# A mixture-of-experts kernel: token pairs fetched one product group earlier, sums of y reordered, constant matmuls in the head

## The chip, the cores and the metric

The kernel runs on one core of a Trainium2 chip. The metric is the device time of one execution in microseconds (us); lower is better. The engines are TensorE (PE), VectorE (DVE), ScalarE (ACT) and GpSimd (POOL); SyncE (SP) only issues DMA transfers.

## The reference

`x` has 4 x 1024 tokens of width 512. A rotation of four 128-wide parts (quaternions, with a gate per channel) is applied to each token, then a mixture of experts: 8 experts, each token goes to its best 2, each expert takes at most 1024 tokens, and its two layers are 512 x 2048 and 2048 x 512.

```python
x_rotated = hamilton(q_left_n, hamilton(x_filtered, q_right_conj))
scores = softmax(xf @ gate_w.T); topv, topi = top_k(scores, 2)
loc = place of the token in its expert; valid = loc < cap
h = relu(einsum('ecd,ehd->ech', de, fc1_w) + fc1_b)
eo = einsum('ech,ehd->ecd', h, fc2_w) + fc2_b
out = x + sum(gathered * gates * w)
```

## The kernel before

Everything is float32, and each product is made of three float32r matmuls: each operand is split in a high part (ACT copies it to float32r) and a low part (DVE subtracts), and high x high, high x low and low x high are added up (L1002 to L1004, L1025 to L1030). The first layer is done by a Strassen-Winograd scheme with seven products instead of eight on 2 x 2 blocks.

**Head** (up to about 118 us): logits, top 2, the slot of each token, and tables of rows (`gather_row`). The tokens of expert 0 are gathered, turned on TensorE, rotated from PSUM (`rotate_ps`, L792) and combined to the sums of y (`y_sum`, L751), of which `y_high` (ACT, L454) and `y_low` (DVE, L767) make the two parts.

**Each expert e** then has 32 steps of the second layer, and 8 groups of the first. A *group* g makes two tiles of the hidden layer: seven `product` calls (six matmuls each), and two calls of `fc2` (twelve each) for tiles of the group before. After the groups come 16 *tiles*, in which TensorE only does `fc2`. In these tiles DVE and ACT also make the sums of y of the next expert. The order of each engine's work is written out by hand in its block; semaphores tie them together.

**Tokens of the next expert** come in four *pairs* of blocks V = 4e .. 4e+3, each two blocks of 128 tokens, through one buffer `x_blk`:

1. POOL gathers the two blocks from `in_x` (`gather_x`, L345), after DVE has turned the pair before (`cut_T`), and writes them to a scratch `slots_dram` in HBM;
2. SP reads them back in another cut, by eight DMAs (`cut_x`, L265, through `load_cut`), once the write has landed (`cut_out`);
3. DVE waits for them (`cut_in`) and transposes them (`turn_x`, L772); ACT makes the first term of the rotation (`first_of_slab`, L469) and DVE adds the three others (`rotate`, L783).

Before the change DVE turns pair 0 in group 0, pair 1 in group 1, pair 2 late in group 4 and pair 3 in group 5. In a group, `turn_x` stands before the sum that releases TensorE's last product (L877, `c22_done`, waited for at L1095):

```python
if g < 2: turn_x(4 * e + g)
...
dve.wait_ge(s3_ready, G + 1)
dve.scalar_tensor_tensor(h1[:, 2 * g + 1, :], ps[:, BANK_P5, :], bias[1], s3[:, :], ...).then_inc(c22_done, 1)
```

SP also loads the weights in one queue: `load_w2` (one DMA each, three buffers; step N+3 is loaded when `w2_ready` shows step N used) and `load_w1` (eight DMAs for a group). The w2 steps 0, 1 and 2 of the next expert are asked for in tiles 13, 14 and 15. POOL's queue also holds `gather_rows` and `scatter_rows` of the output (L365, L372), which add a slab's result to `out`, and the gates.

In the first group of an expert ACT copies the first w2 step to its high part (`w2_high`, L448) before it copies `s3` (L535), for which TensorE's product A22 waits.

## Time and profile before

| | us |
|---|---|
| median of 3 runs (lowest, highest) | 1586.12 (1583.0, 1586.63) |
| the profiled execution's own time | 1586.64 |
| its span in the trace | 1584.9 |

The profile is of one execution. Its first part gives the busy time of each engine, its second the span in 40 slices (busy share in tenths, granted TensorE clock, DMA). TensorE is busy for 1416.6 us (89%), DVE for 1074.1 us (68%), ACT for 709.3 us (45%), POOL for 383.0 us (24%). Matmul records overlap, so that a matmul's 0.39 us is its length and not its distance to the next; distances are read from starts.

### The profile page before, as it was taken

The numbers are of one execution on the slowest core, as the hardware profiler recorded it, in microseconds if no ns is written. First come the engines' busy times: TensorE is split into PE (matmuls) and PEld (weight loads), VectorE is DVE, ScalarE is ACT, GpSimd is POOL, SyncE is SP. The second block draws the span as 40 slices with busy tenths as digits, with TensorE's granted clock in tenths as the row PEclk, the third lists the DMA queues.
The fourth block names the chain that finished last, engine by engine and source line by source line (L and its number), as shares of the span: only waits on it lengthen the run. The fifth ranks groups of instructions, "written<-read, shape, count | busy, mean of one in ns | idle before, by whom it ended". The sixth has DMA issues, their size and how long they took to land.

```text
span 1584.9 us, 17933 instructions
## 1 busy us (share of the span) xinstructions
PE 1416.6 (89%) x6095; PEld 1148.1 (72%) x6095; DVE 1074.1 (68%) x1632; ACT 709.3 (45%) x1072; POOL 383.0 (24%) x322
## 2 busy tenths in 40 slices
PE   8548989979898899979899798989899798999997
PEld 5326867868776778758778587767788587788885
DVE  6786758656685768747686567847587476866543
ACT  5234445434463435444454344634454444544442
POOL 1061112520052210531025200522105310240011
PEclk9667999989999899989999899999999899999999
DMA  8465464564555554564635645555545635354232
GB/s 314 155 146 120 81 137 98 168 141 93 115 135 159 118 125 90 153 162 85 141 106 168 132 94 116 142 151 117 125 93 153 156 81 103 103 167 81 52 94 92
DMA packets 452141, 200.45 MB, mean 126 GB/s; under 512 B 398816, under 2 KB 401001, under 8 KB 450130
## 3 DMA queue, kind: packets, MB, share of 16 engines
q1 hardware_dynamic: 429922, 132.27, 37.4%
q0 software_dynamic: 22128, 67.03, 13.6%
q8 instruction: 49, 0.80, 0.2%
q14 instruction: 42, 0.34, 0.1%
HBM read 159.50 MB, written 39.98 MB: 126 GB/s over the span
## 4 chain that ended last, share of the span: by engine, by line
PE 62%; DVE 14%; DMA 11%; SPq 4%; issue 4%; POOL 3%; ACT 1%; DVEq 0%; POOLq 0%; ACTq 0%
PE ps L1025 11%; PE ps L1026 11%; PE ps L1030 11%; PE ps L1002 9%; PE ps L1004 8%; PE ps L1003 8%; DMA x_blk<-in_x,gather_row 4%; SPq L228 4%; DMA slots_dram<-x_blk 3%; DMA x_blk<-slots_dram 2%; DVE w_lo L745 2%; POOL rows L368 1%; DVE yfull L801 1%; DVE yfull L789 1%; DVE h L816 1%
## 5 line engine op out<-in xcount | busy, mean ns | idle before, releaser
L1002 PE MATMUL ps<-yc_hi,w1c_hi 128*128 128x512 f32 x896 | 360.9, 403 | 103.1 <-DVE h L877 100.7
L1025 PE MATMUL ps<-w_hi,h_hi 128*128 128x512 f32 x960 | 383.3, 399 | 4.1 <-issue 2.4
L1026 PE MATMUL ps<-w_lo,h_hi 128*128 128x512 f32 x960 | 380.2, 396 | 0.0
L1003 PE MATMUL ps<-yc_lo,w1c_hi 128*128 128x512 f32 x896 | 357.7, 399 | 0.0
L1004 PE MATMUL ps<-yc_hi,w1c_lo 128*128 128x512 f32 x896 | 357.7, 399 | 0.0
L1002 PEld LDWEIGHTS ps<-yc_hi,w1c_hi 128*128 128x128 f32 x896 | 173.2, 193 | 147.7 <-DVE h L877 106.6
L1030 PE MATMUL ps<-w_hi,h_lo 128*128 128x512 f32 x960 | 256.8, 389 | 0.0
L1025 PEld LDWEIGHTS ps<-w_hi,h_hi 128*128 128x128 f32 x960 | 186.1, 194 | 49.6 <-issue 5.3
L1026 PEld LDWEIGHTS ps<-w_lo,h_hi 128*128 128x128 f32 x960 | 185.2, 193 | 39.2
L1030 PEld LDWEIGHTS ps<-w_hi,h_lo 128*128 128x128 f32 x960 | 180.5, 188 | 37.9
L1004 PEld LDWEIGHTS ps<-yc_hi,w1c_lo 128*128 128x128 f32 x896 | 173.6, 194 | 37.2
L1003 PEld LDWEIGHTS ps<-yc_lo,w1c_hi 128*128 128x128 f32 x896 | 173.9, 194 | 35.6
L745 DVE TENSOR_TENSOR w_lo<-w_raw,w_hi 128x512 fp32r<-128x512 f32 x256 | 175.4, 685 | 19.2 <-ACT w_hi L452 19.1
L376 POOL DMA_INDIRECT out<-rows,scatter_row x32 | 83.3, 2602 | 416.1 <-DVE rows L816 408.8
L452 ACT ACTIVATE w_hi<-w_raw 128x512 fp32r<-128x512 f32 x256 | 159.7, 624 | 46.4 <-PE ps L1030 41.2
L740 DVE TENSOR_TENSOR w1c_lo<-w1t,w1c_hi 128x1792 fp32r<-128x1792 f32 x64 | 129.6, 2026 | 35.1 <-ACT w1c_hi L446 33.1
L446 ACT ACTIVATE w1c_hi<-w1t 128x1792 fp32r<-128x1792 f32 x64 | 109.2, 1706 | 91.4 <-DVE w1t L736 79.8
L350 POOL DMA_INDIRECT x_blk<-in_x,gather_row x56 | 54.5, 972 | 385.2 <-DVE x_turned L780 361.9
L806 DVE SCALAR_TENSOR_TENSOR h_lo<-ps,h_hi 128x512 fp32r<-128x512 f32 x64 | 44.2, 690 | 138.2 <-ACT h_hi L530 131.3
L780 DVE STREAM_TRANSPOSE x_turned<-x_blk 128x512 f32<-128x512 f32 x56 | 36.5, 690 | 145.7 <-DMA x_blk<-slots_dram 145.7
L789 DVE SCALAR_TENSOR_TENSOR yfull<-x_turned,rot,yfull 128x512 f32<-128x512 f32 x168 | 114.8, 747 | 0.0
L489 ACT ACTIVATE ps<-ps,b1T 128x512 f32<-128x512 f32 x64 | 42.3, 662 | 152.9 <-PE ps L1004 128.5
(160 smaller groups left out, 1578.2 us busy)
## 6 DMA issues: line engine op xcount, KB each, us to landing
w_raw<-in_L_ffn_fc_w SPq DMA_DIRECT2D x256, 256.0 KB
w_raw<-in_L_ffn_fc_w SPq DMA_DIRECT2D x512, 64.0 KB
slots_dram<-x_blk POOLq DMA_DIRECT2D x28, 512.0 KB
x_blk<-slots_dram SPq DMA_DIRECT2D x224, 64.0 KB
out<-x_all SPq DMA_DIRECT2D x8, 1024.0 KB, 12.6
x_all<-in_x SPq DMA_DIRECT2D x7, 1024.0 KB, 13.3
b_bc<-in_L_ffn_fc_b POOLq DMA_DIRECT2D x8, 256.0 KB
x_all<-in_x SPq DMA_DIRECT2D x4, 256.0 KB, 3.9
```

The lines of the kernel that those rows point to most:

```text
L376: pool.indirect_dma_start(out_rows, bass.IndirectOffsetOnAxis(ap=scatter_row[:, at:at + 1], axis=0), slab_rows[s % 2][:, b, :], None, boun ...
L446: act.activation(w1c_hi[:, G % 2, :, :], w1t[:, 1:8, :], ACT.Copy).then_inc(w1_hi_ready, 1)
L452: act.activation(w2_hi[:, N % 3, :], w2_raw[:, N % 3, :], ACT.Copy).then_inc(w2_hi_ready, 1)
L740: dve.tensor_tensor(w1c_lo[:, G % 2, :, :], w1t[:, 1:8, :], w1c_hi[:, G % 2, :, :].bitcast(F32), ALU.subtract).then_inc(w1_ready, 1)
L745: dve.tensor_tensor(w2_lo[:, N % 3, :], w2_raw[:, N % 3, :], w2_hi[:, N % 3, :].bitcast(F32), ALU.subtract).then_inc(w2_ready, 1)
L789: ins = dve.scalar_tensor_tensor(y, x_turned[:, :, j, :], rot[:, i, j:j + 1], y, ALU.mult, ALU.add)
L1002: pe.matmul(bank, hi, yc_hi[:, y, q, :], start=first and q == 0, stop=False, skip_group_check=True)
L1003: pe.matmul(bank, hi, yc_lo[:, y, q, :], start=False, stop=False, skip_group_check=True)
L1004: ins = pe.matmul(bank, lo, yc_hi[:, y, q, :], start=False, stop=last and q == 1, skip_group_check=True)
L1025: pe.matmul(eo_s[:, b, :], h_hi[:, c, blk], w2_hi[:, w, :], start=False, stop=False, skip_group_check=True)
L1026: pe.matmul(eo_s[:, b, :], h_hi[:, c, blk], w2_lo[:, w, :], start=False, stop=False, skip_group_check=True)
L1030: ins = pe.matmul(eo_s[:, b, :], h_lo[:, c, blk], w2_hi[:, w, :], start=False, stop=False, skip_group_check=True)
```

## The change

Parts of it, by place:

- **SP.** From expert 1 on, the reload of pair 1 stands in tile 12 of the expert before, not at the end of group 0. In expert 0 the reloads of pairs 2, 3 and 4 move to group 3, the end of group 5 and tile 1.
- **POOL.** `gather_x(4e+5)` (pair 1 of the next expert) moves in front of `scatter_rows(2e+1)`.
- **DVE.** Pair 0 is turned in tile 10 of the expert before (in the head for expert 0), pair 1 in group 0, pair 2 late in group 3, pair 3 in group 5 as before. In expert 0 these stand one group later (`lag`). The sums of y have another order and other buffers: T3's sum goes to y12, T1's to the turned blocks, T4's to y21; the low parts of B11 and B21 come ahead of sums 1 and 2.
- **ACT.** The first terms of the rotation are made in groups 0 and 5 (1 and 6 in expert 0). In the head the copies for T4 and B22 and the biases of the output banks are made inside group 0.
- **PE.** In the head 28 matmuls whose result nobody reads (`keep_warm`) stand after product p2, and the four that prepare the output banks wait for the rotation only.

```diff
@@ sync
-                    if not last and g == 2:
+                    if not last and g == (2 if e else 3):
                         cut_x(4 * e + 2)
-                    if e < E - 2 and g == 6:
+                    if 0 < e < E - 2 and g == 6:
                         cut_x(4 * e + 4)
...
-                    if not last and g == 0:
-                        cut_x(4 * e + 1)
-                    if not last and g == 4:
+                    if e == 0 and g == 0:
+                        cut_x(1)
+                    if not last and g == (4 if e else 5):
                         cut_x(4 * e + 3)
...
+                    if e == 0 and tile == 1:
+                        cut_x(4)
+                    if e < E - 2 and tile == 12:
+                        cut_x(4 * e + 5)
@@ gpsimd
+                if e == 0:
+                    gather_x(1)
                 if not last:
-                    gather_x(4 * e + 1)
                     gather_x(4 * e + 2)
...
                 gather_rows(2 * e + 1)
+                if e < E - 2:
+                    gather_x(4 * e + 5)
                 scatter_rows(2 * e + 1)
@@ scalar
+                    if G == 0:
+                        y_high(0, T4, 4, y21)
+                        y_high(0, B22, 0, y22)
                     w2_high(N)
...
-                    if not last and g == 1:
+                    if not last and g == (0 if e else 1):
                         first_of_slab(e + 1, 0)
...
                         if tile == 6:
-                            y_high(e + 1, T2, 3, y11)
+                            y_high(e + 1, T2, 2, y11)
                         if tile == 7:
-                            y_high(e + 1, T3, 1, t3)
+                            y_high(e + 1, T3, 3, y12)
@@ vector
             rotate_ps(1)
+            rotate_ps(2)
             y_low(0, B11, y11)
             y_low(0, B21, y21)
-            rotate_ps(2)
             rotate_ps(3)
...
+            turn_x(0)
...
+                    lag = 0 if e else 1
                     if not last:
-                        if g < 2:
-                            turn_x(4 * e + g)
-                        elif g < 5:
-                            rotate(e + 1, 0, g - 1)
-                        elif g == 5:
+                        if g == lag:
+                            turn_x(4 * e + 1)
+                        if lag < g < 4 + lag:
+                            rotate(e + 1, 0, g - lag)
+                        if g == 5 + lag:
                             turn_x(4 * e + 3)
...
-                    if not last and g == 4:
+                    if not last and g == 3 + lag:
                         turn_x(4 * e + 2)
...
                         if tile == 1:
+                            if lag:
+                                rotate(e + 1, 1, 3)
                             y_sum(e + 1, 0)
...
-                        if tile == 3:
+                        if tile == 5:
                             y_sum(e + 1, 1)
...
-                        if tile == 5:
+                        if tile == 6:
                             y_sum(e + 1, 2)
...
+                        if tile == 10 and e < E - 2:
+                            turn_x(4 * e + 4)
@@ tensor
                     if G == 0:
                         p2(G)
+                        keep_warm(28)
+                        pe.wait_ge(rotated, rotated_by(0, 1, 6))
+                        set_bits(range(EO[0], EO[0] + SB))
```

POOL's queue around the end of expert 1, before. The first row is the scatter of the first slab, then come the bias row, the gather and scatter of the second slab's rows, the gather for the next expert's first slab, and a pair of token blocks with its write.

```order
L376 DMA out<-rows,scatter_row 4096x512 x4
L384 DMA b_bc<-in_L_ffn_fc_b 128x512
L368 DMA h<-out,gather_row 128x512 x4
L376 DMA out<-h,scatter_row 4096x512 x4
L368 DMA rows<-out,gather_row 128x512 x4
L350 DMA x_blk<-in_x,gather_row 128x512 x2
L355 DMA slots_dram<-x_blk 128x2x512
```

The same place with the change:

```order
L380 DMA out<-rows,scatter_row 4096x512 x4
L388 DMA b_bc<-in_L_ffn_fc_b 128x512
L372 DMA h<-out,gather_row 128x512 x4
L354 DMA x_blk<-in_x,gather_row 128x512 x2
L359 DMA slots_dram<-x_blk 128x2x512
L380 DMA out<-h,scatter_row 4096x512 x4
L372 DMA rows<-out,gather_row 128x512 x4
```

The pair's two gathers and its write have moved ahead of the second slab's scatter, behind the four gathers of `h`.

SP's queue at the turn from expert 1 to expert 2, before: 18 w2 loads (16 in the tiles, of which the last three are the next expert's steps 0, 1 and 2, and 2 in its group 0), then group 0's w1, the reload of pair 1, and group 1's loads.

```order
L263 DMA w_raw<-in_L_ffn_fc_w 128x512 x18
L228 DMA w_raw<-in_L_ffn_fc_w 32x16x32 x8
L228 DMA x_blk<-slots_dram 32x16x32 x8
L263 DMA w_raw<-in_L_ffn_fc_w 128x512 x2
L228 DMA w_raw<-in_L_ffn_fc_w 32x16x32 x8
```

With the change:

```order
L263 DMA w_raw<-in_L_ffn_fc_w 128x512 x13
L228 DMA x_blk<-slots_dram 32x16x32 x8
L263 DMA w_raw<-in_L_ffn_fc_w 128x512 x5
L228 DMA w_raw<-in_L_ffn_fc_w 32x16x32 x8
L263 DMA w_raw<-in_L_ffn_fc_w 128x512 x2
```

The reload of pair 1 now stands in front of the last five w2 loads, three of which are the next expert's steps 0, 1 and 2.

DVE in tiles 5, 6 and 7 of expert 1, before (L806 and L745 are the low parts of h and w2 that each tile needs; L761 is `y_sum` 2, L769 a `y_low`):

```order
L806 SCALAR_TENSOR_TENSOR h_lo<-h,h_hi 128x512
L745 TENSOR_TENSOR w_lo<-w_raw,w_hi 128x512
L761 TENSOR_TENSOR yfull<-yfull 128x2x512
L806 SCALAR_TENSOR_TENSOR h_lo<-h,h_hi 128x512
L745 TENSOR_TENSOR w_lo<-w_raw,w_hi 128x512
L769 TENSOR_TENSOR yc_lo<-yfull,yc_hi 128x1024
```

With the change (L816 and L754 are these low parts, L768 is `y_sum` 1, L771 `y_sum` 2):

```order
L816 SCALAR_TENSOR_TENSOR h_lo<-h,h_hi 128x512
L754 TENSOR_TENSOR w_lo<-w_raw,w_hi 128x512
L768 TENSOR_TENSOR yfull<-yfull,x_turned 128x2x512
L816 SCALAR_TENSOR_TENSOR h_lo<-h,h_hi 128x512
L754 TENSOR_TENSOR w_lo<-w_raw,w_hi 128x512
L771 TENSOR_TENSOR yfull<-yfull 128x2x512
```

A sum stands in tile 6 as well, where a low part stood; ACT's copy of its result stands in tile 7.

## Rows read from the trace of the kernel before

**Rows 1.** The page, part 2: the span in 40 slices.

```profile
PEclk9667999989999899989999899999999899999999
...
GB/s 314 155 146 120 81 137 98 168 141 93 115 135 159 118 125 90 153 162 85 141 106 168 132 94 116 142 151 117 125 93 153 156 81 103 103 167 81 52 94 92
```

**Rows 2.** Waits of PE over the span: us in total, times, longest us.

```profile
PE ps L1002 <- DVE h L877: 100.7, 14, 11.4
```

**Rows 3.** Busy times by stretch: expert 1, and expert 7 (clock is next to last).

```profile
303.00:487.00 184.00, 168.44 (x720) 137.50 (x719) 127.11 (x187) 84.54 (x127) 48.18 (x37) 0.95 0.55 128
...
1408.00:1571.50 163.50, 163.50 (x723) 135.40 (x723) 85.97 (x130) 68.70 (x106) 18.50 (x16) 1.00 0.35 89
```

**Rows 4.** Timeline of PE, expert 1: start, us, what [idle before <- releaser].

```profile
335.58 0.79 PE L1002 MATMUL ps<-yc_hi,w1c_hi 128*128 128x512 f32 x1 [10.24 <-DVE h L877]
...
339.10 0.39 PE L1025 MATMUL ps<-w_hi,h_hi 128*128 128x512 f32 x1
...
402.08 0.79 PE L1002 MATMUL ps<-yc_hi,w1c_hi 128*128 128x512 f32 x1 [4.75 <-DVE h L877]
...
407.34 0.39 PE L1025 MATMUL ps<-w_hi,h_hi 128*128 128x512 f32 x1
```

**Rows 5.** Timeline of DVE, expert 1, the turns of pairs 1 and 3.

```profile
333.59 1.30 DVE L780 STREAM_TRANSPOSE x_turned<-x_blk 128x512 f32<-128x512 f32 x2 [12.53 <-DMA x_blk<-slots_dram]
...
400.09 1.30 DVE L780 STREAM_TRANSPOSE x_turned<-x_blk 128x512 f32<-128x512 f32 x2 [8.88 <-DMA x_blk<-slots_dram]
```

**Rows 6.** Timelines of POOL and SP, expert 1: gather, write, reload.

```profile
322.94 0.76 POOL L355 DMA_DIRECT2D slots_dram<-x_blk  x1 [5.60 <-DMA x_blk<-in_x,gather_row]
...
382.52 0.95 POOL L350 DMA_INDIRECT x_blk<-in_x,gather_row  x1 [29.28 <-DVE x_turned L780]
...
389.46 0.75 POOL L355 DMA_DIRECT2D slots_dram<-x_blk  x1 [4.74 <-DMA x_blk<-in_x,gather_row]
...
326.15 5.55 SPq L228 DMA_DIRECT2D x_blk<-slots_dram  x8
```

**Rows 7.** Timelines of PE and SP, head and expert 0.

```profile
118.44 2.08 PE L1036 MATMUL ps<-yc_hi,w1c_hi 128*128 128x512 f32 x4 [9.97 <-DVE yc_lo L769]
...
148.88 0.80 PE L1002 MATMUL ps<-yc_hi,w1c_hi 128*128 128x512 f32 x1 [4.44 <-DVE h L877]
...
217.84 0.80 PE L1002 MATMUL ps<-yc_hi,w1c_hi 128*128 128x512 f32 x1 [6.11 <-DVE h L877]
...
138.64 5.72 SPq L228 DMA_DIRECT2D x_blk<-slots_dram  x8
```

**Rows 8.** Timelines of DVE, ACT and PE, expert 1: rotation, tiles 6 and 7.

```profile
441.14 2.73 DVE L789 SCALAR_TENSOR_TENSOR yfull<-x_turned,rot,yfull 128x512 f32<-128x512 f32 x4
...
458.77 0.69 DVE L806 SCALAR_TENSOR_TENSOR h_lo<-h,h_hi 128x512 fp32r<-128x512 f32 x1 [1.70 <-ACT h_hi L583]
...
457.16 1.06 ACT L460 ACTIVATE yc_hi<-yfull 128x1024 fp32r<-128x1024 f32 x1 [5.36 <-DVE yfull L761]
...
462.98 0.39 PE L1025 MATMUL ps<-w_hi,h_hi 128*128 128x512 f32 x1
```

**Rows 9.** Timelines of POOL and DVE, expert 1, tiles 8 to 12.

```profile
464.91 6.54 POOL L368 DMA_INDIRECT h<-out,gather_row  x1 [0.30 <-issue]
...
473.01 1.36 POOL L368 DMA_INDIRECT h<-out,gather_row  x1 [0.30 <-issue]
...
472.26 0.69 DVE L806 SCALAR_TENSOR_TENSOR h_lo<-h,h_hi 128x512 fp32r<-128x512 f32 x1 [1.70 <-ACT h_hi L583]
...
474.77 0.69 DVE L806 SCALAR_TENSOR_TENSOR h_lo<-h,h_hi 128x512 fp32r<-128x512 f32 x1 [1.22 <-ACT h_hi L583]
```

**Rows 10.** Timelines of PE and ACT, expert 1, group 0.

```profile
303.17 0.39 PE L1002 MATMUL ps<-yc_hi,w1c_hi 128*128 128x512 f32 x1
...
312.81 0.47 PE L1002 MATMUL ps<-yc_hi,w1c_hi 128*128 128x512 f32 x1
...
309.31 0.62 ACT L452 ACTIVATE w_hi<-w_raw 128x512 fp32r<-128x512 f32 x1
```

More of the change, by code:

```diff
@@ L167, in program @@
         x0_rows = h1[:, 0:2 * SB, :]
-        t3 = x_turned[:, 0:2, :, :].rearrange("p b q n -> p (b q n)").rearrange("p (k n) -> p k n", k=2)
+        t1 = x_turned[:, 0:2, :, :].rearrange("p b q n -> p (b q n)").rearrange("p (k n) -> p k n", k=2)
         slab_rows = (rows[:, :, :], h1[:, ROWS1:ROWS1 + SB, :])
@@ L506, in _ @@
             seed_c11(0)
-            y_high(0, T2, 3, y11)
-            y_high(0, T3, 1, t3)
-            y_high(0, T1, 2, y12)
-            act.wait_ge(bits_set, 2)
-            for b in range(SB):
-                seed_eo(0, b)
-            y_high(0, T4, 4, y12)
-            y_high(0, B22, 0, y22)
+            y_high(0, T2, 2, y11)
+            y_high(0, T3, 3, y12)
+            y_high(0, T1, 1, t1)
             for e in range(E):
@@ L536, in _ @@
                     w2_high(N + 1)
+                    if G == 0:
+                        act.wait_ge(bits_set, 2)
+                        for b in range(SB):
+                            seed_eo(0, b)
                     if g < GROUPS - 1:
@@ L551, in _ @@
                         w1_high(G + 2)
-                    if not last and g == 1:
+                    if not last and g == (0 if e else 1):
                         first_of_slab(e + 1, 0)
-                    if not last and g == 5:
+                    if not last and g == (5 if e else 6):
                         first_of_slab(e + 1, 1)
@@ L774, in turn_x @@
                 if u == 0:
-                    dve.wait_ge(yc_ready, 7 * e)
+                    dve.wait_ge(yc_ready, 7 * (e - 1) + T1 + 1)
                 if u == 2:
@@ L1037, in set_bits, with keep_warm @@
                 ins.then_inc(bits_set, 1)
+            def keep_warm(count):
+                for n in range(count):
+                    pe.matmul(ps[:, BANK_P5, :], w1c_hi[:, 0, A11, 0:P], yc_hi[:, B11, 0, :], start=True, stop=True)
             def p1(G):
@@ L1065, in _ @@
                         p2(G)
+                        keep_warm(28)
+                        pe.wait_ge(rotated, rotated_by(0, 1, 6))
+                        set_bits(range(EO[0], EO[0] + SB))
                     if g == 0:
                         pe.wait_ge(yc_ready, 7 * e + T2 + 1)
-                    if G == 0:
-                        set_bits(range(EO[0], EO[0] + SB))
                     pe.wait_ge(c11_seeded, G + 1)
```

45 lines of the change are left out of this document (22 added, 23 removed).

## The prediction, made before the change was run

> **What bounds the kernel now.** I read the clock and rate by slice first, then PE's waits, then the stretches of single experts, then the timelines around the longest waits. The granted clock [rows 1] is at 0.9 or more nearly everywhere, with dips of 0.8 that come twice per expert. PE's waits [rows 2] have one large entry: 14 waits, 100.7 us in all, for DVE's sum at L877. Fourteen is two for each of the seven experts that fetch tokens for a next one. The stretches [rows 3] (behind each total come PE, PEld, DVE, ACT and POOL busy, then clock, DMA share and GB/s) show the price: expert 1 does its 720 matmuls in 184 us at a clock of 0.95, expert 7, which fetches nothing, does 723 in 163.5 at 1.00. That is 0.2267 us from start to start, so 163.2 us is the floor of an expert and some 21 us of each are lost. PE bounds the kernel, and what it waits for decides.
>
> In expert 1 PE stops for 10.24 us in group 1 and 4.75 us in group 5 [rows 4]. DVE at these places waits 12.53 and 8.88 us at the head of a turn, for the reload from the scratch [rows 5]; the sum at L877 stands behind it in DVE's queue. So DVE has 2.3 us of slack in group 1 and 4.1 us in group 5. The fetch itself is a chain [rows 6]: from the first gather (382.52) to the write (389.46) 6.9 us, longer when other gathers are in the queue; 3.2 us from the write (322.94) to the reload's start (326.15); 5.55 us to issue its eight DMAs, and the data are there at 333.59 [rows 5], 7.4 us after that start. About 18 us in all, against a group of 15 us (66 matmuls). After each stop the clock is low: the eight matmuls from 335.58 to 339.10 take 3.5 us instead of 1.8, and the twelve from 402.08 to 407.34 take 5.3 instead of 2.7 [rows 4]. That adds 1.7 and 2.5 us.
>
> **What the change removes.** In experts 1 to 6 pair 1 is asked for in group 0, but its buffer is free since tile 10 of the expert before; that stop goes from group 1. Pair 2 is turned late in group 3, pair 3 in group 5, so pair 3 has nearly two groups. Its reload now comes out behind group 4's w1 in SP's queue. By my chain w1 is issued from 381.7 to 387.4 in the old trace's time, the reload starts there, lands at 394.9, and DVE asks at 391.2: a wait of 3.7 us against the slack of 4.1 us [rows 4, 5]. I take 0.3 us for PE, between 0 and 1.
> Stops removed: 100.7 minus the 4.44 of expert 0's group 1 [rows 7], which stays: **96.3**. Low clock behind them: 6 x (1.7 + 2.5) + 2.5 for expert 0's group 6: **27.7**.
>
> **The head and expert 0.** Pair 1 of expert 0 is still asked for in group 1; its fetch starts when pair 0 is turned, now at the end of the head. DVE no longer waits 1.1 us for ACT's copies between the rotations, and the sums need less waiting, so T2's parts are ready some 2.3 us sooner. PE can't use all of it: one preparing matmul, 18 of products (7.1 us from about 105) and the 28 constant ones (6.35 us at full clock) end at 118.5, and the four that prepare banks at 119.4, where before they ended at 120.5 at low clock [rows 7]. But then PE goes on at full clock, and the biases are out of its way. Step by step the turn of pair 0 ends 2 us sooner, the w1 loads start 3.1 us sooner, and with them the reload that now starts at 138.64 [rows 7]. So PE's stop in group 1 remains and ends **3.1** us sooner. If the constant matmuls ran at low clock they would end 6 us later, and this gain would be a loss of about 3; if they cost nothing the gain is 4.
>
> **What it adds.**
> *Tiles.* Today the copy for T2 waits for a sum, and DVE then waits 1.70 us for ACT's h copy of tile 6 [rows 8]. With the sums in tiles 5 and 6, the same happens again in tile 7: the sum ends at 461.2, ACT copies T3 (1.06 us [rows 8]) and then h (0.6), and DVE has both low parts of tile 7 at 464.2, when PE wants them at 462.98 [rows 8]. In tile 11 the turn of pair 0 fills an idle stretch of DVE and costs nothing beside 0.2 us. I take 1.3 us in each of seven experts, between 0 and 2: **9.1**. In expert 0 one rotation (2.73 us [rows 8]) comes into the tiles, where DVE has no slack (PE already waits there for a quarter of a us): **2.9**. Pair 3 costs 7 x 0.3 = **2.1**.
> *The turn of experts.* This is the step that decides. POOL's gathers of pair 1 come behind the four of `h`. In these tiles a POOL gather that starts while DVE runs without a gap is held: one of 0.95 us takes 6.54, from 464.91 to 471.45, and DVE's run ended 0.9 us before, ahead of the gap in front of 472.26; one at 473.01 takes 1.36 and ends as long after that run's end [rows 9]. With the change DVE's runs are from 462.9 to 472.4, 474.05 to 475.3, and 476.55 to 483.7. POOL's four gathers of `h` end at 477.4, the pair's first at 478.7 (it starts as the first instructions of the last run end), and the second, at 479.0, falls into the middle of the run and is held till 484.6. The write starts at 489, and the reload at 492.3, 3.4 us after the next expert's first matmul (488.9, with the tiles' delay).
> SP stands still at this reload, and behind it are the loads of the next expert's w2 steps 0, 1, 2. Its issue takes 5.5 us, its data 7.4 us, and the 256 KB of step 0 another 1.0 (between 0.8 and 2.1, at the 314 and 126 GB/s of the slices and their mean [rows 1]). So step 0 lands 11.8 us into the expert. ACT asks for it 6.14 us in (309.31 against 303.17 [rows 10]) and has `s3` queued behind it. `s3` is then ready at 13.1; PE wants it at 8.2 for A22: a stop of 5.0 us. That is as long as the one of 4.75, so I add 2.4 us of low clock. DVE's low part, turn and L877 follow by 15.2, while A22 runs slow till 15.7, so they add nothing; the last product began at 9.64 before (312.81 [rows 10]). ACT's first term, which moves into group 0 (2.56 us), hides in this delay. 7.4 us in each of six experts: **44.4**. Ends: 2.3 us where no gather is held, 14 us where everything is late.
> The Trainium skill, "SBUF — State Buffer", "Who interferes with whom", says that a DVE instruction with two SBUF inputs and a GpSimd instruction that reads SBUF exclude each other, the second being blocked until the first finishes. By that rule the hold would last for one DVE instruction and not for a run, and the second rival's time would come out; this trace shows holds of whole runs [rows 9].
>
> **The sum.** 96.3 + 27.7 + 3.1 = 127.1 gained; 9.1 + 2.9 + 2.1 + 44.4 = 58.5 given back; 68.6 net. The profiled execution's own time is 1586.64 (its span is 1584.9; the median of the runs is 0.5 lower): 1586.6 - 68.6 = **1518 us**. Of the parts at no cost: the moved transposes and first terms are as many as before; their cover is DVE's and ACT's idle time in the groups, and without it each pair would cost 1.3 us and each first term 2.56.
>
> **The rivals.**
> 1. *The forecast*, one gather held: 1518, its own range 1506 to 1530. Chance 0.50.
> 2. *No gather is held longer than one DVE instruction.* The write starts about 4.3 us sooner, the reload ahead of the next expert, w2 lands 7.4 us in. The stop is 1.1 us at full clock, and the first term moved into group 0 shows with 1.2 us, since `s2` of group 1 is late. 2.3 instead of 7.4 us: 6 x 5.1 = 30.6 less, 1487. For it: gathers at the start of a run pass after one instruction; against: those in the middle did not. Chance 0.23.
> 3. *Both are held*, one behind the other: 1.3 us more each turn, 1526. Chance 0.12.
> 4. *The change doesn't do what it says*: pair 1's data come as late as now and w2 behind them, 14 us per turn instead of 7.4: 1558. For it: pair 1 then lies on a chain with no spare group. Chance 0.09.
> 5. *Slower: the weights behind the reload.* The same mechanism turns the sign when w2's first step lands 68.6 / 6 = 11.4 us later still, 23 us into the expert. It needs two holds of 6.5 us in a row. With 13 us more for each turn the time is 1596. Against: DVE is idle behind tile 15, so a second hold ends there. Chance 0.03.
> About 0.03 is left for what I don't see, half of it slower or the same.
>
> **The numbers.** The range leaves out rival 5 and the high end of 4, and takes in rival 2 with a tile stage that costs nothing: 1482 to 1545. A difference of 0.3% (4.8 us) is about what a measurement of this kernel can tell from none. Faster by more: 0.95, within it: 0.01, slower: 0.04.
>
> **What would show it.** Right: PE's waits for the sum at L877's place fall from 100.7 us to under 15; new waits of about 5 us in group 0 of experts 1 to 6, for ACT's `s3`, which waited for a w2 load; POOL's second pair gather at the turn takes 5 us or more; an expert takes 173 to 175 us; 28 matmuls end near 118.5 at full clock. Wrong: stretches of experts 1 to 6 under 168 us (rival 2), or a wait for `x_turned` in group 0 (rival 4), or a PE wait of several us in group 5.

## The result and the profile after the change

| | us |
|---|---|
| median with the change, 4 runs (lowest, highest) | 1480.5 (1479.55, 1481.15) |
| median before, 4 runs beside them (lowest, highest) | 1586.38 (1583.0, 1591.39) |
| ratio, 95% interval | 0.933 (0.930 to 0.936) |
| the profiled execution's own time, its span | 1480.76, 1479.0 |

The change makes the kernel 105.9 us faster. I had forecast 68.6 us, 1518 with a range from 1482 to 1545; the time lies 1.5 us below its low end.

The page's second part, the span in 40 slices, answers [rows 1]:

```profile
PEclk9659999999999999999999999999999999999999
...
GB/s 302 191 139 107 119 105 120 172 181 112 126 116 203 117 132 104 172 181 112 125 109 199 136 114 114 172 178 114 129 102 185 151 108 79 151 137 68 50 110 81
```

The dips to 0.8 in the middle of the span are gone. Waits of PE over the span (us, times, longest) answer [rows 2]:

```profile
PE ps L1041 <- DVE w_lo L754: 14.5, 22, 2.4
...
PE ps L1018 <- DVE h L889: 8.7, 3, 6.4
...
PE ps L1018 <- ACT s L528: 6.5, 7, 1.0
```

The wait for the sum (now L889) fell from 100.7 to 8.7 us, of which 6.4 are expert 0's stop in group 1. The waits for `w_lo` have grown (1.7 us in all before), and new is one per expert for `s2` (L528). The stretches of expert 1 and expert 7 answer [rows 3]:

```profile
297.20:465.10 167.90, 165.26 (x722) 134.64 (x721) 127.46 (x188) 84.34 (x127) 47.18 (x37) 1.00 0.58 140
1304.00:1467.70 163.70, 163.58 (x722) 135.18 (x720) 86.47 (x132) 68.62 (x106) 17.46 (x17) 1.00 0.35 89
```

Expert 1 went from 184 to 167.9 us and its clock from 0.95 to 1.00; expert 7 did not change. In the trace of after, expert 1's first product starts at 297.42, before at 303.17. Split at such starts (the first and the last product of each expert), the profiled executions give this table, in us:

| piece | before | after | gained | forecast |
|---|---|---|---|---|
| up to expert 1's first product | 303.2 | 297.4 | 5.8 | 7.2 |
| groups of experts 1 to 6, mean | 131.4 | 113.0 | 18.4 | 11.5 |
| tiles of experts 1 to 6, mean | 53.1 | 54.8 | -1.7 | -1.3 |
| expert 7 | 163.4 | 163.4 | 0 | 0 |

5.8 + 6 x (18.4 - 1.7) = 106. The head, the tiles and expert 7 are near the forecast. (My 11.5 are 15.0 of stops and 4.2 of low clock, less 0.3 for pair 3 and 7.4 for the turn; my 7.2 are 3.1, 6.1 and 2.5, less 0.3, 1.3 and 2.9.) The groups gain 6.9 us per expert more than I gave them, 41 us in all. The miss is 37.3 us: the tiles and the head took back the rest.

So the question is the turn of experts, my term of 44.4 us. The timeline of POOL in expert 1 with the change, tiles 4 to 13, answers [rows 9]:

```profile
426.42 7.69 POOL L380 DMA_INDIRECT out<-rows,scatter_row  x1 [0.31 <-DVE rows L826]
...
440.91 1.43 POOL L372 DMA_INDIRECT h<-out,gather_row  x1 [0.31 <-issue]
442.65 2.00 POOL L372 DMA_INDIRECT h<-out,gather_row  x1 [0.30 <-issue]
444.96 2.01 POOL L372 DMA_INDIRECT h<-out,gather_row  x1 [0.31 <-issue]
447.28 0.94 POOL L372 DMA_INDIRECT h<-out,gather_row  x1 [0.30 <-issue]
450.01 0.94 POOL L354 DMA_INDIRECT x_blk<-in_x,gather_row  x1 [1.79 <-DVE x_turned L790]
451.26 1.07 POOL L354 DMA_INDIRECT x_blk<-in_x,gather_row  x1 [0.30 <-issue]
455.75 0.76 POOL L359 DMA_DIRECT2D slots_dram<-x_blk  x1 [3.42 <-DMA x_blk<-in_x,gather_row]
```

By a *run* of DVE I mean instructions without a gap between them; an issue of POOL, some 0.95 us alone, is *held* when it lasts over more than the DVE instruction in which it starts, and is *let go* where it ends, 0.8 to 0.9 us behind the end of a DVE instruction. The scatter at 426.42 is held to the end of a run, as before. The first gather of `h`, which took 6.54 us before, takes 1.43. Neither gather of pair 1 is held. SP then issues the reload, and the w2 loads behind it:

```profile
458.99 5.33 SPq L228 DMA_DIRECT2D x_blk<-slots_dram  x8
464.35 11.39 SPq L263 DMA_DIRECT2D w_raw<-in_L_ffn_fc_w  x5
```

The next expert begins at 465.31. The reload starts 6.3 us ahead of it; I had put it 3.4 us behind. ACT's row for the first w2 step shows no wait, and what is left of the turn is one wait of PE in group 1, for `s2`, which stands behind the first term that moved into group 0:

```profile
471.44 0.62 ACT L459 ACTIVATE w_hi<-w_raw 128x512 fp32r<-128x512 f32 x1
```

```profile
482.94 0.50 PE L1018 MATMUL ps<-yc_hi,w1c_hi 128*128 128x512 f32 x1 [0.94 <-ACT s L528]
```

In the tiles DVE waits for ACT twice, where [rows 8] show it once, and PE stops behind the second (timelines of DVE and PE, tiles 6 and 7 of expert 1):

```profile
434.92 0.69 DVE L816 SCALAR_TENSOR_TENSOR h_lo<-h,h_hi 128x512 fp32r<-128x512 f32 x1 [1.69 <-ACT h_hi L592]
...
439.05 0.69 DVE L816 SCALAR_TENSOR_TENSOR h_lo<-h,h_hi 128x512 fp32r<-128x512 f32 x1 [1.70 <-ACT h_hi L592]
```

```profile
440.39 0.50 PE L1041 MATMUL ps<-w_hi,h_hi 128*128 128x512 f32 x1 [1.11 <-DVE w_lo L754]
```

The head and expert 0, to compare with [rows 7]:

```profile
112.28 6.51 PE L1058 MATMUL ps<-yc_hi,w1c_hi 128*128 128x512 f32 x28
118.63 1.07 PE L1052 MATMUL ps<-yc_hi,w1c_hi 128*128 128x512 f32 x4
121.83 0.47 PE L1018 MATMUL ps<-yc_hi,w1c_hi 128*128 128x512 f32 x1 [0.78 <-ACT s L528]
...
147.58 0.79 PE L1018 MATMUL ps<-yc_hi,w1c_hi 128*128 128x512 f32 x1 [6.37 <-DVE h L889]
```

The 28 constant matmuls end where I put them, at full clock. The stop of group 1 ends at 147.58 and not at 148.88, 1.3 us sooner where I had 3.1.

### The profile page after: what moved, and what is told of

It reads as the page before. It is cut to its first block and busy times, and to the rows that moved or that the text cites. A ratio compares the mean times of both kernels' runs of the same rounds, so it can differ in the third digit from the quotient of the medians.

```text
span 1479.0 us, 17990 instructions
## 1 busy us (share of the span) xinstructions
PE 1393.7 (94%) x6123; PEld 1128.6 (76%) x6123; DVE 1074.4 (73%) x1632; ACT 707.3 (48%) x1072; POOL 369.2 (25%) x322
## 5 line engine op out<-in xcount | busy, mean ns | idle before, releaser
L1041 PE MATMUL ps<-w_hi,h_hi 128*128 128x512 f32 x960 | 377.5, 393 | 14.6 <-DVE w_lo L754 14.5
L1042 PE MATMUL ps<-w_lo,h_hi 128*128 128x512 f32 x960 | 374.4, 390 | 0.0
L1018 PE MATMUL ps<-yc_hi,w1c_hi 128*128 128x512 f32 x896 | 352.2, 393 | 15.6 <-DVE h L889 8.7
L1019 PE MATMUL ps<-yc_lo,w1c_hi 128*128 128x512 f32 x896 | 350.2, 391 | 0.0
L1020 PE MATMUL ps<-yc_hi,w1c_lo 128*128 128x512 f32 x896 | 350.1, 391 | 0.0
L1041 PEld LDWEIGHTS ps<-w_hi,h_hi 128*128 128x128 f32 x960 | 180.6, 188 | 63.8 <-DVE w_lo L754 26.8
L1042 PEld LDWEIGHTS ps<-w_lo,h_hi 128*128 128x128 f32 x960 | 180.5, 188 | 36.9
L1020 PEld LDWEIGHTS ps<-yc_hi,w1c_lo 128*128 128x128 f32 x896 | 169.1, 189 | 35.6
L1019 PEld LDWEIGHTS ps<-yc_lo,w1c_hi 128*128 128x128 f32 x896 | 169.2, 189 | 34.5
L754 DVE TENSOR_TENSOR w_lo<-w_raw,w_hi 128x512 fp32r<-128x512 f32 x256 | 174.8, 683 | 19.6 <-ACT w_hi L459 19.6
L816 DVE SCALAR_TENSOR_TENSOR h_lo<-ps,h_hi 128x512 fp32r<-128x512 f32 x64 | 44.2, 690 | 135.8 <-ACT h_hi L532 135.8
L816 DVE SCALAR_TENSOR_TENSOR h_lo<-h,h_hi 128x512 fp32r<-128x512 f32 x128 | 87.7, 685 | 38.4 <-ACT h_hi L592 38.4
```

The source lines that it names most:

```text
L754: dve.tensor_tensor(w2_lo[:, N % 3, :], w2_raw[:, N % 3, :], w2_hi[:, N % 3, :].bitcast(F32), ALU.subtract).then_inc(w2_ready, 1)
L816: dve.scalar_tensor_tensor(h_lo[:, N % 4, :], full, 0.0, h_hi[:, N % 4, :].bitcast(F32), ALU.max, ALU.subtract).then_inc(h_ready, 1)
L1018: pe.matmul(bank, hi, yc_hi[:, y, q, :], start=first and q == 0, stop=False, skip_group_check=True)
L1019: pe.matmul(bank, hi, yc_lo[:, y, q, :], start=False, stop=False, skip_group_check=True)
L1020: ins = pe.matmul(bank, lo, yc_hi[:, y, q, :], start=False, stop=last and q == 1, skip_group_check=True)
L1041: pe.matmul(eo_s[:, b, :], h_hi[:, c, blk], w2_hi[:, w, :], start=False, stop=False, skip_group_check=True)
```

## The experiments

All are edits of the changed kernel, and their times are compared with its 1480.5 us. They come from three other sets of runs, in which the kernel before took 1592.2, 1586.4 and 1591.6 us (medians; the ratios given are to these). In the third a kernel that differs from the changed one in the place of one small load only took 1480.3.

### The old order of the sums

The first experiment asks whether POOL's holds come back with the order that DVE had before, and what the new order costs in the tiles.

```diff
@@ vector, tiles, experts 1 to 7 (ACT's copies name the same buffers)
-                        if tile == 3:
-                            y_low(e + 1, B11, y11)
-                        if tile == 4:
-                            y_low(e + 1, B21, y21)
-                        if tile == 5:
-                            y_sum(e + 1, 1)
-                        if tile == 6:
-                            y_sum(e + 1, 2)
+                        if tile == 3:
+                            y_sum(e + 1, 1)
+                        if tile == 4:
+                            y_low(e + 1, B11, y11)
+                        if tile == 5:
+                            y_sum(e + 1, 2)
+                        if tile == 6:
+                            y_low(e + 1, B21, y21)
```

> The changed kernel with the old order of the y sums in the tiles (T3's sum first, one sum each in tiles 3 and 5, none in 6), the head and everything else as changed. The changed kernel takes 1480.5 us; its tiles take 55.2 us per expert from the last product to the next expert's first, 53.5 before. Theory A (a POOL gather is held for DVE's whole run, and the old order brings the hold back): the tiles cost 1.7 us less in each of seven experts, 12 us, but POOL's first gather of h takes about 6.5 us again (1.4 and 2.0 with the change), pair 1's second gather is held too, the reload starts 3 us after the next expert's first product and PE stops for about 5 us in group 0: 6 x 5 to 7.4 = 30 to 44 us more, 1499 to 1513 us in all. Theory B (no gather that matters is held, or a hold doesn't reach the weights): only the tiles change, 1468.5 us (1466 to 1471), and no wait over 1.5 us in group 0. Theory C (the second wait of DVE for ACT in tile 7 isn't what costs 1.7 us, the turn in tile 10 is): 1480 us and tiles of 55.

Measured: 1478.8 us (1476.1 to 1479.8), ratio to before 0.929 (0.925 to 0.932). The tiles take 53.1 us in experts 1 to 6 and 56.3 in expert 0, 1.7 us less in each of seven, as A and B have it. The groups of experts 1 to 6 take 114.7 us on the average, 1.7 more than with the change. Timeline of POOL in expert 1:

```profile
440.51 6.79 POOL L372 DMA_INDIRECT h<-out,gather_row  x1 [0.31 <-issue]
...
453.05 1.43 POOL L354 DMA_INDIRECT x_blk<-in_x,gather_row  x1 [0.30 <-issue]
```

Half of A is right: the hold of the gather of `h` is back, in each of experts 0 to 6 (4.6 to 6.8 us), and the order of DVE's and ACT's work is what brings it. It ends at 447.30, 0.9 us behind a sum of y, though DVE goes on without a gap into the turn of pair 0 (timeline of DVE):

```profile
445.22 1.22 DVE L776 TENSOR_TENSOR yfull<-yfull 128x1024 f32<-128x1024 f32 x1
446.35 1.29 DVE L806 STREAM_TRANSPOSE x_turned<-x_blk 128x512 f32<-128x512 f32 x2
```

But pair 1's second gather is still not held, and here it does start in the middle of a run: 2.4 us into one of ten instructions (450.64 to 457.98), inside the fourth, after which it is let go. The reload starts at 461.00, 2.4 us ahead of the next expert's first product at 463.4, and ACT gets step 0 at 471.03:

```profile
471.03 0.63 ACT L459 ACTIVATE w_hi<-w_raw 128x512 fp32r<-128x512 f32 x1 [1.42 <-DMA w_raw<-in_L_ffn_fc_w]
```

Waits of PE in expert 2:

```profile
PE ps L1034 <- ACT s L528: 1.0, 1, 1.0
PE ps L1034 <- ACT s L540: 0.6, 1, 0.6
PE ps L1034 <- DVE h L905: 0.5, 1, 0.5
```

So a turn of experts with one hold costs some 1.7 us more, neither the 5 to 7.4 of A nor the nothing of B.

### The weights ahead of the reload

If those 1.7 us are w2 behind the reload, they go when the queue's order is turned round.

```diff
-                    if e < E - 2 and tile == 12:
+                    if e < E - 2 and tile == 15:
                         cut_x(4 * e + 5)
```

> e1_old_sums (1478.8 us) with the reload of pair 1 in tile 15 of SP's queue, behind the next expert's w2 steps 0, 1 and 2, and not in tile 12 ahead of them. In e1_old_sums the groups of experts 1 to 6 take 114.5 us on the average and 112.9 with the change. Theory A (those 1.6 to 1.8 us are w2's step 0 behind the reload, 0.6 to 2.0 us of waits for ACT's s3 each): they go, 6 x 1.7 = 10 us less, 1468.5 us (1467 to 1470), the wait for s3 in group 0 under 0.3 us, groups of 112.9. Rival B (pair 1's data come too late instead, its reload issues last and shares the DMA rate with the weights): a wait for the sum behind its turn in group 0, 1 to 3 us, 1475 to 1485 us.

Measured: 1470.1 us (1469.1 to 1470.8), 8.7 less than with the old sums alone and 10.4 less than the changed kernel. In the traces the groups of experts 1 to 6 take 113.3 us on the average, 1.4 less than with the old sums alone. The queue of SP around the turn:

```profile
440.61 17.53 SPq L263 DMA_DIRECT2D w_raw<-in_L_ffn_fc_w  x8
462.21 5.42 SPq L228 DMA_DIRECT2D x_blk<-slots_dram  x8
```

The w2 steps are all issued before the reload can go. PE's waits for `s3` are gone in expert 2 (0.9 us for `s2` stay), and its groups take 112.8 us. Rival B shows a little: PE waits 1.7 us for a sum in expert 1, whose groups take 114.5 us, and those of expert 5 take 113.9; with these the time is 1.6 us above A's number. The waits for `s3` went with the turned order and nothing else was edited, so the price was the weights behind the reload.

### The reload made late on purpose

The same mechanism at a high dose, which is my fifth rival, the one on the slower side.

```diff
-                if e < E - 2:
-                    gather_x(4 * e + 5)
                 scatter_rows(2 * e + 1)
+                if e < E - 2:
+                    gather_x(4 * e + 5)
```

> The changed kernel with pair 1's gathers and write behind the scatter of the second slab in POOL's queue; the place of its reload in SP's queue stays (tile 12, ahead of the next expert's w2 steps). Theory A (my price for weights that stand behind the reload: PE stops by the landing of step 0 plus 1.3 minus 8.2 us, plus 2.4 us of low clock): the scatter's four issues end 4.8 us into the expert, the write starts about 10 us into it, the reload about 13.4, and by e1_old_sums (reload at 461.0, w2 used at 471.0) step 0 is used 10.0 us behind that, 23.4 us into the expert: a stop of 16.5 us and 2.4 of low clock, less the wait of 1.0 there now, 18 us in each of six experts, 1588 us (1575 to 1600); PE waits for ACT's s3. Theory B (weights aren't delayed by a reload that waits, only x_turned is): PE waits for the sum behind pair 1's turn, 486 against 475 wanted, 11 to 13 us, 1550 to 1570 us. Theory C (there is slack that I don't see): under 1540 us.

Measured: 1594.4 us (1591.7 to 1597.1), ratio to before 1.005 (1.003 to 1.007). Expert 2's first product is at 484.6; SP's reload, ACT's row, and PE's waits in expert 2:

```profile
499.95 6.55 SPq L228 DMA_DIRECT2D x_blk<-slots_dram  x8
```

```profile
509.91 0.63 ACT L459 ACTIVATE w_hi<-w_raw 128x512 fp32r<-128x512 f32 x1 [19.07 <-DMA w_raw<-in_L_ffn_fc_w]
```

```profile
PE ps L1018 <- ACT s L540: 18.2, 1, 18.2
```

The reload started 15.3 us into the expert and step 0 was used at 25.3, again 10.0 us behind the reload's start. The rule "landing plus 1.3 minus 8.2" gives 18.4 us; PE stopped for 18.2. The price that I put on late weights holds at 7.6 us (0.7 by the rule, 0.6 measured) and at 25.3. What failed was the time of landing that I put in. The groups of experts 1 to 6 take 131.8 us, 18.8 more than with the change: the 18.2, less the 0.9 for `s2` that is gone, and so some 1.5 us of low clock where I had put 2.4. This edit of one place takes back all of the gain.

### Pair 1 ahead of the gathers of h

```diff
@@ gpsimd, and the old order of the sums as above
+                if e < E - 2:
+                    gather_x(4 * e + 5)
                 pool.wait_ge(h_ready, e * STEPS + HT + ROWS1 + SB)
                 gather_rows(2 * e + 1)
-                if e < E - 2:
-                    gather_x(4 * e + 5)
```

> The old order of the y sums in the tiles as in e1_old_sums, and the two gathers of pair 1 and its write ahead of the four gathers of h in POOL's queue, directly behind the turn of pair 0 in tile 10. Theory A (what decides is whether the reload of pair 1 goes out before the weights' turn, and a hold of POOL's gathers is what delays it): whatever e1_old_sums gives, here the write starts about 9 us before the next expert and the reload 5 us before it, so 1468.5 us (1466 to 1471) and e1_old_sums 30 us or more above. Theory B (holds don't matter): both 1468.5 us within 1.5. Rival C (the gathers of h now come too late for the sum of the second slab, whose release PE waits for in group 0): a wait for that sum at the first products of groups 0 and 1, 1 to 5 us per expert, 1475 to 1500 us.

Measured: 1495.4 us (1489.4 to 1496.5; the profiled execution is the one of 1489.4). Neither A nor B, but C. The write goes out at 452.82, 11.7 us ahead of the next expert, but the gathers of `h` end at 459.5 and the second slab's sum waits for them; PE waits for that sum in the next expert (L842):

```profile
PE ps L1034 <- DVE h L842: 4.7, 2, 2.5
```

The order of POOL's queue that the change chose, rows first and tokens behind, is the better one.

### When the gathers of h start

```diff
-                scatter_rows(2 * e)
                 if not last:
                     load_b2(e + 1)
+                scatter_rows(2 * e)
```

> The changed kernel with the load of the bias row ahead of the first slab's scatter in POOL's queue, so that the gathers of h start some 0.9 us sooner, at about 440.0 us in expert 1 and not at 440.91, in the middle of the same run of DVE. Theory A (whether POOL's gather is held for the whole run depends on the moment at which it starts): the first gather of h takes 5 us or more, as in e1_old_sums (6.79). Theory B (it depends on what DVE has queued, so on the order of the sums): it takes under 2.5 us, as with the change (1.43, 2.00, 2.01). The time says little: 1480.5 us within 1 by B, up to 1490 by A.

Measured: 1480.3 us (1478.9 to 1481.7).

```profile
441.30 1.79 POOL L372 DMA_INDIRECT h<-out,gather_row  x1 [3.48 <-DVE h_lo L816]
443.39 2.01 POOL L372 DMA_INDIRECT h<-out,gather_row  x1 [0.30 <-issue]
```

B holds, though the test is weaker than meant: DVE's run began at 439.79 and not at 439.05, and the gather started 1.5 us into it and not 1.9. With the new order no gather of `h` took more than 2.02 us, in any expert of this kernel.

### Pair 3 one group later

```diff
-                    if not last and g == 3 + lag:
+                    if not last and g == 4:
                         turn_x(4 * e + 2)
```

> The changed kernel with pair 2 turned late in group 4 of every expert, as before the change, and so pair 3 asked for one group later; pair 1 stays one group ahead. Theory A (the schedule of pair 3 alone took away the stop of group 5, 4.75 us, and 2.5 us of low clock, and nothing hides it): these come back in experts 1 to 6, 6 x 7.25 = 43 us more, 1524 us (1518 to 1528), and a wait for the sum behind the turn in group 5. Expert 0 is the same in both. Rival B (the stop of group 5 was a follow-up of the one in group 1, through the reload's place behind loads that came late): 1481 to 1500 us.

Measured: 1521.2 us (1518.2 to 1523.7), 40.7 more. In the profiled execution the groups of experts 1 to 6 take 119.4 us, 6.4 more. Waits of PE in expert 2:

```profile
PE ps L1018 <- DVE h L889: 4.3, 1, 4.3
```

A holds: 40.7 / 6 = 6.8 us for each expert against the 7.25 of stop and low clock in [rows 4]. Pair 3's new schedule is worth two fifths of the gain.

### Pair 1 as before

Pair 1 is gathered and reloaded in its own expert again, and the first slab's work stands one group later in every expert, as in expert 0 (only a part of the edit is shown).

```diff
-                    lag = 0 if e else 1
+                    lag = 1
@@ gpsimd, sync
-                    if e < E - 2 and tile == 12:
-                        cut_x(4 * e + 5)
...
-                    if e == 0 and g == 0:
-                        cut_x(1)
+                    if not last and g == 0:
+                        cut_x(4 * e + 1)
```

> The changed kernel with expert 0's schedule in all experts: pair 1 is gathered behind the scatter of the second slab and reloaded at the end of group 0, as before the change, everything else of the first slab stands one group later, and one rotation goes into the tiles. Theory A (pair 1 one group ahead takes away the stop of group 1, 10.24 us and 1.7 of low clock in experts 1 to 6, and a rotation in the tiles costs the 3.3 us by which expert 0's tiles, 58.1, are longer than the others' 54.8): 6 x (11.9 + 3.3) = 91 us more, 1571 us (1565 to 1577), a wait of about 10 us for the sum in group 1. Rival B (in expert 0 that stop is 6.4 us and 2.2 of low clock; the early turn of pair 0 alone shortens it in all experts): 6 x (8.6 + 3.3) = 71 us more, 1552 us.

Measured: 1576.3 us (1575.6 to 1577.0), 95.8 more, against 91 by A.

```profile
331.66 0.79 PE L1011 MATMUL ps<-yc_hi,w1c_hi 128*128 128x512 f32 x1 [11.49 <-DVE h L882]
```

This row of PE is the stop in group 1 of expert 1, 11.5 us; the expert's groups take 125.6 us and its tiles 58.1. Over experts 1 to 6 the groups take 12.6 us more each and the tiles 3.3, 76 and 20 us. So the early turn of pair 0 alone is worth nothing in experts 1 to 6: the stop goes only when pair 1 is asked for in the expert before. Pair 1 makes the larger part of the gain.

### The head: no constant matmuls, and 18 of them

```diff
-                        keep_warm(28)
```

> The changed kernel without the 28 constant matmuls in the head; their result is read by nobody. Theory A (my term for the head): PE stands idle for the 6.4 us that they take, since the rotation is ready no sooner, and then runs at the 1.2 GHz level for some 10 us as before the change (118.4 to 130.5 us); of that loss of up to 5 us the group 1 stop takes up what is not on the chain of w1 loads and reload, so 1482 to 1485 us. Theory B (all of it disappears in the stop of 6.4 us in group 1): 1480.5 us within 0.7, and a stop in group 1 that is shorter by as much as PE comes later. Theory C (they hold PE up): 1479 us or less, the four preparing matmuls start before 118 us.

Measured: 1478.7 us (1476.9 to 1478.9), 1.8 less than with them: C. In the traces expert 1's first product comes 1.4 us sooner (296.0, 297.4). Without them the product behind starts when T2's low part is ready, though PE then runs at the 1.2 GHz level (clock 0.50 in this stretch):

```profile
116.76 0.79 PE L1018 MATMUL ps<-yc_hi,w1c_hi 128*128 128x512 f32 x1 [3.74 <-issue]
```

```profile
118.60:125.70 7.10, 6.32 (x15) 4.46 (x14) 5.42 (x7) 5.79 (x10) 0.07 (x1) 0.50 0.07 28
```

The 28 and the four preparing ones occupied PE until 119.5, 2.8 us beyond that. The gap from 112.9 to 116.8 has room for 18. The next edit takes 18, and puts them behind the four preparing ones:

```diff
-                        keep_warm(28)
                         pe.wait_ge(rotated, rotated_by(0, 1, 6))
                         set_bits(range(EO[0], EO[0] + SB))
+                        keep_warm(18)
```

> The changed kernel with 18 constant matmuls in the place of 28, and the four that prepare the banks ahead of them. Without any (e3_no_constant, 1478.7 us) the product behind them starts at 116.76 and not 119.5, since T2's low part is ready at 116.7, but PE runs at the 1.2 GHz level until 125.7. Theory A (28 are too many: they hold PE 2.7 us past T2, but the clock that they keep is worth up to 3): with 18, which end at 116.8, both are had: S2 starts near 116.9 at full clock, S3 waits for s2 until about 119.2, the group 1 stop ends 2 to 3 us sooner than with the change, 1477.5 to 1478.5 us. Theory B (behind e3_no_constant nothing is left, the chain is DVE's and ACT's): 1478.7 us within 0.4. Theory C (the four matmuls and their wait matter): 1480 us or more.

Measured: 1477.7 us (1477.3 to 1478.5), 2.8 less than with 28. The number and the place were changed together and not each by itself.

```profile
112.87 4.25 PE L1058 MATMUL ps<-yc_hi,w1c_hi 128*128 128x512 f32 x18
116.96 0.39 PE L1018 MATMUL ps<-yc_hi,w1c_hi 128*128 128x512 f32 x1
...
119.29 0.47 PE L1018 MATMUL ps<-yc_hi,w1c_hi 128*128 128x512 f32 x1 [0.78 <-ACT s L528]
```

S3 starts at 119.29 where it started at 121.83, and the clock stays at full. Against the 28 the gain of 2.8 us is clear, and A's number. Against none it is 1.0 us with ranges that overlap, so that B is not excluded by the times alone; expert 1's first product, at 295.1 and 296.0 us in the two profiled executions, says the same as the times.

### Expert 0's pair 1 turned at the end of group 1

```diff
@@ vector
-                        if g == lag:
+                        if e and g == 0:
                             turn_x(4 * e + 1)
-                        if lag < g < 4 + lag:
+                        if lag < g < 4 + lag and G != 2:
...
                     w2_low(N + 1)
+                    if G == 2:
+                        rotate(1, 0, 1)
...
                         w1_low(G + 2)
+                    if G == 1:
+                        turn_x(1)
@@ scalar
                     w2_high(N)
+                    if G == 2:
+                        first_of_slab(1, 0)
```

> The changed kernel with one move in expert 0: pair 1 is turned at the end of group 1 and no longer ahead of the sum that releases PE's last product; ACT's first term goes into group 2 ahead of s3, and the first of the rotations behind that sum in group 2. Theory A (the stop of 6.4 us in group 1 is DVE's queue alone, and the data have time until group 2): the stop goes, and with it the low clock from 145.1 to 152.0 us, in which about 4.4 us ran at half speed, 2.2 us: 8.6 us less, 1472 us (1470 to 1474). Rival B (the wait moves: ACT's s2 of group 2 stands behind the first part of w1, which waits for DVE, and S3 waits for it): a new wait of 2 to 4 us in group 2 and 1475 to 1479 us. Rival C (pair 2 and 3 of expert 0 are fetched later by as much, and a stop comes back in group 4 to 6): 1479 to 1483 us.

Measured: 1471.8 us (1471.4 to 1472.5), 8.7 less, as A has it. DVE's sum and the turn:

```profile
139.15 0.75 DVE L891 SCALAR_TENSOR_TENSOR h<-ps,b1T,s 128x512 f32<-128x512 f32 x1 [1.56 <-PE ps L1026]
...
147.39 1.31 DVE L792 STREAM_TRANSPOSE x_turned<-x_blk 128x512 f32<-128x512 f32 x2 [0.28 <-DMA x_blk<-slots_dram]
```

The sum goes out 8.2 us ahead of the turn that it used to wait for, and by then the data are nearly there: DVE waits 0.28 us for them, not 8.6.

### The edits together

The old sums, the reload in tile 15, the late turn in expert 0 and the 18 matmuls, as shown above.

> Four edits of the changed kernel together: the old order of the sums in the tiles and the reload of pair 1 in tile 15 (e6_weights_first, 1470.1 us), the late turn of pair 1 in expert 0 (e2_late_turn, 8.7 us less), and 18 constant matmuls behind the four preparing ones (e7_constant_18, 2.8 us less, of which the start of expert 1 shows 2.3). If the effects add up, since they lie in the tiles, at the turn of experts, in group 1 of expert 0 and in the head: 1470.1 - 8.7 - 2.5 = 1458.9 us (1457.5 to 1460.5). Rival (the sooner head only makes the wait for pair 1's data longer, which the late turn no longer hides): 1461.5 us or more, with a wait in group 1 or 2 of expert 0.

Measured: 1458.3 us (1457.1 to 1459.7), ratio to before 0.916 (0.913 to 0.918), 22.2 less than the changed kernel. The effects add up. Waits of PE from 120 us (expert 0) to 460 (expert 2's first group):

```profile
PE ps L1063 <- DVE w_lo L756: 2.6, 2, 2.4
PE ps L1040 <- DVE h L907: 2.3, 2, 1.9
PE ps L1040 <- ACT s L528: 0.9, 1, 0.9
```

## Why the prediction was right, and where it was wrong

**Stops removed, 96.3 us, and the low clock behind them, 27.7.** Right. PE's wait for the sum fell by 92.0 us over the whole span, of which expert 0's stop grew by 2 and a wait of 1.9 in its group 0 is new. PE's busy time fell from 1416.6 to 1393.7 us although the 28 matmuls added 6.5 to it, so 29.4 us of low clock went. Pair 3 made 6.8 us per expert, by its experiment.

**Pair 3's own wait, 0.3 us for each expert.** It did not come; the waits of experts 1 and 2 show none for the sum.

**The head, 3.1 us sooner.** Direction right, size 1.3. I traced the path through DVE and SP and let PE end at 118.5, but did not ask when the product behind the constant matmuls could have begun: at 116.8, by the experiment without them. They kept the clock and took 2.8 us for it.

**Tiles, 1.3 us in each of seven experts.** Measured 1.7, and taking the new order back gave just that. The mechanism (a sum in tile 6 sets up a second wait of DVE for ACT in tile 7) is the one in the text. The rotation in expert 0's tiles cost 3.3 us, not 2.9.

**The turn of experts, 44.4 us.** This is the step that failed. Measured is one wait of 0.9 us for `s2` in each expert, 6 x 0.9 = 5.4 us. "Step 0 lands 11.8 us into the expert" was wrong: it was there before ACT asked, 6.1 us in.

Two things had gone into the landing, both holds of POOL. (1) I let the first gather of `h` be held for the rest of DVE's run as in [rows 9]. The new order of the sums ended that, and with the old order it is back, 6.79 us.

(2) "The second falls into the middle of the run and is held till 484.6" is wrong. With the change that gather starts in the last instruction of a run and takes 1.07 us; with the old sums it does start in the middle of one, and takes 1.43. With hold (1) alone the reload starts 2.4 us ahead of the next expert, without it 6.3 ahead, and I had 3.4 behind: of the 9.7 us by which I had it too late 3.9 are hold (1), and most of the other 5.8 the hold (2), 4.6 us in my times, that never came. I had made a rule out of the few rows of [rows 9], that what starts in the middle of a run is held to its end. The same trace shows otherwise in expert 6, in a row that I left out of account (timelines of POOL and DVE before the change):

```profile
1383.86 1.43 POOL L376 DMA_INDIRECT out<-rows,scatter_row  x1 [0.30 <-issue]
...
1381.40 0.69 DVE L806 SCALAR_TENSOR_TENSOR h_lo<-h,h_hi 128x512 fp32r<-128x512 f32 x1 [1.70 <-ACT h_hi L583]
...
1383.75 0.69 DVE L806 SCALAR_TENSOR_TENSOR h_lo<-h,h_hi 128x512 fp32r<-128x512 f32 x1
```

This scatter starts 2.5 us into a run of 15 instructions (1381.40 to 1393.19), inside the fourth, and is let go after that one: the very place at which I let the second gather start, 479.0 in a run from 476.55. One more number had the other sign: from the reload's start to the use of step 0 I took 8.4 us, and 10.0 were measured, so a reload at my 3.4 would have cost 1.6 us more than I said (an estimate from these two). The price of a landing, by contrast, was right: 0.6 us at a landing of 7.6, 18.2 at 25.3.

**The range.** Its low end was to be the second rival with tiles that cost nothing. That is 1487.4 - 9.1 = 1478.3 us and not the 1482 that I wrote. The measured 1480.5 would then have been inside, but by luck: the tiles cost more than I said and the turn less.

**The rivals.** The second rival, in which no gather is held longer than one instruction, is what happened to the gathers; one scatter in each expert was held. It foresaw that the moved first term shows in group 1 through `s2`, with 1.2 us (0.9 measured). Its 1487 us were 6.5 too many: it still let the reload start about 1 us ahead of the next expert, where it started 6.3 ahead, since I had let the hold of `h` stand in it (its write came 4.3 us sooner, the second hold alone), and took from that a stop of 1.1 us in each expert. By the Trainium skill, "SBUF — State Buffer", "Who interferes with whom", a DVE instruction with two SBUF inputs and a GpSimd instruction that reads SBUF contend for one lock, and the one that comes second is blocked until the other finishes. For the gathers of `h` with the change that describes the rows: those at 442.65 and 444.96 end 0.8 us behind the end of the DVE instruction in which they start. The scatter at 426.42, of 7.69 us, went on to the end of the eighth instruction after the one in which it started, in the same trace, and does not agree. The fifth rival's mechanism is real, and one move in POOL's queue from here: 1594.4 us against its 1596.

What stays open is why some transfers of POOL are held over many instructions of DVE and others are let go after one. I looked at how far ACT was ahead: at the gather at 464.91 of the old trace ACT's next `w_hi` was finished 2.1 us before DVE used it, at those of 442.65 and 444.96 of the new one 1.8 us before. But the gather at 445.71 in the experiment with the bias row was let go with 2.5 us, and one in the kernel with four edits (1094.31, 5.30 us) was held with 1.4, so that is no rule. Nor is it how far DVE's run has come: 5.9 us into a run one gather was held (440.51 with the old sums, run from 434.65) and one let go (444.96 with the change, run from 439.05). I have no rule. One thing is the same throughout: in the tiles of the 13 traces 120 gathers and scatters of output rows took over 2.6 us, and every one was let go behind a sum of y, never behind a low part. Behind these sums DVE waits 1.7 us or goes on to a turn, and which of these matters was not tested.

## What to carry to other kernels

Where a load waits in a queue for something slow, look at what stands behind it: moving one reload behind three loads was worth 8.7 us, and moving its source behind one slab's scatter cost 114 us. A wait at the head of an in-order engine is often cheapest to take away by moving the waiting instruction behind the one that others want, as the late turn in expert 0 shows. And a hold seen in a trace is tied to the order of both engines there: look through the whole trace for a case at the same place that was not held, and when the change touches that order, give "no hold" and "hold" equal weight and work each through to the landing.

## What the runs showed of the hardware that I had not expected

- Whether a POOL gather is held over many DVE instructions changes with the order of DVE's instructions and ACT's copies, with the same kinds of instructions: with the new order of the sums no gather of `h` took over 2.03 us in eight kernels, with the old one of them took 4.6 to 6.8 us in each of seven experts of four kernels. The place of the gathers matters too: with the old order, but the pair ahead of them, only one of 32 was held (5.30 us). A hold ends 0.8 to 0.9 us behind the end of a DVE instruction in all of them.
- From the start of the eight reload DMAs to the use of the w2 step that is issued behind them it took 10.0 us in two kernels (461.00 to 471.03, and 499.95 to 509.91). I had worked with 8.4.
- Constant matmuls that keep the clock up can cost more than the low clock: with 28 of them the kernel was 1.8 us slower than with none (1.4 us by the start of expert 1 in the traces), with 18, which end just as the next operand is ready, 2.8 us faster than with 28.
